# Rows of the fifth and sixth expert block transposed by VectorE and moved by DMA, table of late blocks and loads moved up

## What is computed

```python
# x, ctx_1024: (32, 128, 256) f32
x = x + xattn(ctx_1024, layernorm(x))      # 16 heads of 64, keys and values over ctx and x rows
h = layernorm(x)                           # (4096, 256)
assign = argmax(h @ centroids.T)           # one of 8 experts for each token
xhat = layernorm(h)
y = h + relu((xhat * ln_g[e] + ln_b[e]) @ w1[e].T + b1[e]) @ w2[e].T + b2[e]
alpha = sigmoid(h . centroids[e])
out = x + alpha * y + (1 - alpha) * h      # e = assign of the token
```

## Time and profile before

| | before |
|---|---|
| median of 3 runs | 1053.27 us (1052.5 to 1053.7) |
| profiled execution | 1052.73 us |
| its span, first to last instruction | 1050.9 us |
| granted TensorE clock, mean | 0.999 |
| PE busy | 1041.6 us, 99% |
| DVE busy | 844.9 us, 80% |
| ACT busy | 688.7 us, 66% |
| POOL busy | 565.3 us, 54% |
| DMA | 190.57 MB, mean 181 GB/s |

### The profile page before, as it was taken

The page is one execution under the profiler, slowest core; times in us unless marked ns, Lnnn a source line. Parts: engine busy times, 40 slices in busy tenths (PEclk is TensorE's granted clock), DMA queues, the critical chain, the costliest instruction groups (busy, mean ns, idle before and its releaser), DMA issues.

```text
span 1050.9 us, 24670 instructions
## 1 busy us (share of the span) xinstructions
PE 1041.6 (99%) x8610; PEld 940.5 (89%) x8610; DVE 844.9 (80%) x1979; ACT 688.7 (66%) x1838; POOL 565.3 (54%) x665
## 2 busy tenths in 40 slices
PE   9999999999999999999999999999999999999997
PEld 7889898988888888889898989889888999999997
DVE  7878888878888888888888879888887797767663
ACT  6765757675666767666757575766566666676761
POOL 1744464646454555545464646465444667566663
PEclk9999999999999999999999999999999999999999
DMA  6665657585757576767667585856356868777760
GB/s 212 160 169 148 170 156 189 146 215 142 201 146 197 142 193 155 200 156 197 159 168 185 142 210 137 213 144 171 91 153 196 307 198 294 250 234 234 249 194 31
DMA packets 159666, 190.57 MB, mean 181 GB/s; under 512 B 17454, under 2 KB 149038, under 8 KB 154673
## 3 DMA queue, kind: packets, MB, share of 16 engines
q1 hardware_dynamic: 155088, 179.09, 62.4%
q0 software_dynamic: 3360, 8.53, 2.2%
q10 hardware_dynamic: 1088, 1.31, 0.4%
HBM read 65.72 MB, written 46.07 MB: 106 GB/s over the span
## 4 chain that ended last, share of the span: by engine, by line
PE 96%; DVE 2%; POOL 1%; ACT 1%; DMA 0%; issue 0%; POOLq 0%; DVEq 0%
PE psum L742 17%; PE psum L775 16%; PE psum L812 11%; PE psum L902 10%; PE psum L791 10%; PE psum L827 9%; PE psum L761 8%; PE psum L938 6%; PE psum L932 5%; PE psum L830 1%; PE psum L883 1%; PE psum L914 1%; DVE neg_max L1410 1%; DMA c_in<-in_ctx_in 0%; PE psum L856 0%; DVE w_lo L1545 0%
## 5 line engine op out<-in xcount | busy, mean ns | idle before, releaser
L1823 POOL TENSOR_TENSOR prob<-prob,inv_sum 128x512 f32<-128x512 f32 x172 | 177.7, 1047 | 190.1 <-DVE inv_sum L1416 189.2
L1133 ACT ACTIVATE prob<-psum,neg_max 128x256 f32<-128x256 f32 x344 | 160.2, 478 | 38.8 <-DVE neg_max L1410 38.5
L1410 DVE TENSOR_REDUCE neg_max<-psum 128x2 f32<-128x512 f32 x256 | 161.9, 672 | 27.7 <-PE psum L791 27.5
L1422 DVE STREAM_TRANSPOSE prob<-prob 128x512 f32<-128x512 f32 x172 | 118.5, 698 | 12.3 <-POOL prob L1823 11.9
L1823 POOL TENSOR_TENSOR w_ring<-w_ring,inv_sum 128x512 f32<-128x512 f32 x76 | 78.1, 1041 | 76.0 <-DVE inv_sum L1416 75.7
L1140 ACT ACTIVATE head_out_hi<-psum 128x512 fp32r<-128x512 f32 x52 | 31.1, 597 | 105.6 <-PE psum L812 102.4
L1119 ACT ACTIVATE v_n<-psum 128x512 f32<-128x512 f32 x128 | 77.9, 608 | 26.7 <-PE psum L775 22.7
L1108 ACT ACTIVATE k_hi<-psum 128x512 fp32r<-128x512 f32 x128 | 77.0, 603 | 22.0 <-PE psum L742 21.3
L1461 DVE TENSOR_TENSOR k_lo<-psum,k_hi 128x512 fp32r<-128x512 f32 x128 | 85.7, 674 | 0.0
L742 PE MATMUL psum<-kv_t_hi,w_hi 128*128 128x512 f32 x252 | 85.0, 419 | 0.0
L775 PE MATMUL psum<-w_hi,kv_t_hi 128*128 128x512 f32 x256 | 80.2, 395 | 0.4 <-DVE k_lo L1461 0.4
(11 more groups left out here) (215 smaller groups left out, 2952.4 us busy)
## 6 DMA issues: line engine op xcount, KB each, us to landing
sorted_rows<-filler SPq DMA_DIRECT2D x54, 660.0 KB
prob_t<-prob SPq DMA_DIRECT2D x172, 128.0 KB, 2.8
w_ring<-prob SPq DMA_DIRECT2D x172, 128.0 KB, 2.7
w<-in_experts SPq DMA_DIRECT2D x19, 1024.0 KB, 7.8
w_ring<-in_experts SPq DMA_DIRECT2D x18, 1024.0 KB, 6.7
prob_t<-w_ring SPq DMA_DIRECT2D x76, 128.0 KB, 2.8
w_ring<-w_ring SPq DMA_DIRECT2D x76, 128.0 KB, 2.7
w_ring<-normed SPq DMA_DIRECT2D x56, 128.0 KB, 3.0
```

The costliest lines, as they stand in the source:

```text
L1133: act.activation(prob_at(u, bb)[:, :, parity, i], scores_i, ACT.Exp, bias=neg_max[:, at, i:i + 1], accum_out=prob_sum[:, at, i:i + 1]).the ...
L1410: dve.tensor_reduce(neg_max[:, (4 * u + n) % 8, :], psum[:, n, :].rearrange("p (i j) -> p i j", i=2), AXIS_X, ALU.max, negate=True).then_i ...
L1422: dve.transpose(probs, probs).then_inc(s_quad, 1)
L1823: pool.tensor_tensor(probs, probs, inverse, ALU.mult).then_inc(s_soft, 1)
```

## The change

TensorE's transposes of blocks 4 and 5 go; these two blocks take the way of the later ones. `transpose_rows(4)` stands after `split_xn(3)` on VectorE, `transpose_rows(5)` after `split_hidden(3)`. `late_blocks()` moves up: before `low_weights_1(4)` instead of after `split_xn(4)`; `split_xn(4)` comes ahead of `split_hidden(3)`. On SyncE, `move_rows(4)` stands between the loads of block 5's first weights and block 4's second weights; the loads of the rows of blocks 6 and 7, which need the late table, come before `move_rows(5)`, the first weights of block 6, and the second weights of block 5. In `bank_order` two `ft` entries become `pass` entries.

```diff
+FIRST_MOVED = 4
 def bank_order:
-    order += [("ft", 3), ("fy", 1, 0), ("fy", 1, 1), ("rank", n_pairs - 1), ("total",), ("ft", 4),
-              ("fy", 2, 0), ("fy", 2, 1)]
-    for slot in range(3, n_slots):
-        order += [("ft", slot + 2) if slot + 2 < n_early else ("pass", slot, 0), ("fy", slot, 0), ("fy", slot, 1), ("pass", slot, 1)]
+    order += [("ft", 3), ("fy", 1, 0), ("fy", 1, 1), ("rank", n_pairs - 1), ("total",)]
+    for slot in range(2, n_slots):
+        order += [("pass", slot, 0), ("fy", slot, 0), ("fy", slot, 1), ("pass", slot, 1)]
 wait_rows_moved, move_rows, normalise_rows, row_gain_bias, split_xn:
-    ... n_early ...
+    ... FIRST_MOVED ...
 SyncE, for s in range(2, n_early):
                     load_weights_1(s)
+                    if s == n_early - 1:
+                        move_rows(FIRST_MOVED)
                     load_weights_2(s - 1)
                     load_b2(s - 1)
-                load_weights_2(n_early - 1)
-                load_b2(n_early - 1)
                 scattered(n_batches)
                 run = block_steps(sp, count_empty(sp))
                 run(n_early, (load_rows,), (load_vectors,))
                 run(n_early + 1, (load_rows,))
+                for s in range(FIRST_MOVED + 1, n_early):
+                    move_rows(s)
                 run(n_early, (load_weights_1,))
+                load_weights_2(n_early - 1)
+                load_b2(n_early - 1)
                 run(n_early + 1, (load_weights_1,))
 TensorE:
                 layer_1(3)
-                row_transposes(4)
                 layer_2_split(2)
                 for s in range(3, n_early):
                     layer_1(s + 1)
-                    if s + 2 < n_early:
-                        row_transposes(s + 2)
                     layer_2_split(s)
 VectorE:
                 split_xn(3)
+                transpose_rows(4)
                 finish(1)
                 read_ranks(n_pairs - 1)
                 places(n_batches - 2)
                 places(n_batches - 1)
+                late_blocks()
                 low_weights_1(4)
+                split_xn(4)
                 split_hidden(3)
-                split_xn(4)
-                late_blocks()
+                transpose_rows(5)
                 finish(2)
                 for s in range(3, n_early):
-                    if s + 2 == n_early:
-                        transpose_rows(s + 2)
                     low_weights_1(s + 2)
                     split_hidden(s + 1)
                     split_xn(s + 2)
-                    if s + 3 > n_early:
-                        transpose_rows(s + 3)
+                    transpose_rows(s + 3)
                     finish(s)
```

More of the change, by code:

```diff
@@ L35, with bank_order @@
 NW, NW2, NR, NBLOCK = 2, 3, 4, 7
+FIRST_MOVED = 4
 FIRST_SPLIT = 1
 W_OUT_PIECES = 4
-def bank_order(n_pairs, last_of_early, n_early, n_slots):
+def bank_order(n_pairs, last_of_early, n_slots):
     n_steps = 4 * n_pairs
@@ L129, in build @@
     assert last_of_early % 2 == 1
-    assert 5 <= n_early <= n_sure - 2
-    order = bank_order(n_pairs, last_of_early, n_early, n_slots)
+    assert FIRST_MOVED + 2 <= n_early <= n_sure - 2
+    order = bank_order(n_pairs, last_of_early, n_slots)
     number = {item: i for i, item in enumerate(order)}
@@ L446, in wait_rows_moved @@
             def wait_rows_moved(eng, s):
-                eng.wait_ge(f_xm[s % 2], 4 * 16 * ((s - n_early) // 2 + 1))
+                eng.wait_ge(f_xm[s % 2], 4 * 16 * ((s - FIRST_MOVED) // 2 + 1))
             def wait_high(eng, g, side):
@@ L547, in move_rows @@
                 def move_rows(s):
-                    sp.wait_ge(f_xt, s - n_early + 1)
-                    if s == n_early:
+                    sp.wait_ge(f_xt, s - FIRST_MOVED + 1)
+                    if s == FIRST_MOVED:
                         wait_made(sp, ("wout", n_batches - 1))
                     else:
-                        sp.wait_ge(f_g, s - n_early)
+                        sp.wait_ge(f_g, s - FIRST_MOVED)
                     for a in range(4):
@@ L1175, in normalise_rows @@
                         wait_inputs_moved(act, n_pairs - 1)
-                    elif s < n_early + 2:
+                    elif s < FIRST_MOVED + 2:
                         wait_made(act, ("ft", s - 2))
@@ L1182, in normalise_rows @@
                         src, dst = row[:, 0:d_model], xhat[:, s % 2, i, :]
-                        if s >= n_early:
+                        if s >= FIRST_MOVED:
                             src = src.rearrange("p (c k j) -> p j c k", c=KC, j=4)
@@ L1191, in row_gain_bias @@
                     item = ("ft", s)
-                    if s < n_early:
+                    if s < FIRST_MOVED:
                         wait_made(act, item)
@@ L1622, in split_xn @@
                 def split_xn(s):
-                    if s < n_early:
+                    if s < FIRST_MOVED:
                         wait_read(dve, ("ft", s))
                     else:
-                        dve.wait_ge(f_g, s - n_early + 1)
+                        dve.wait_ge(f_g, s - FIRST_MOVED + 1)
                     if s >= 3:
```

## The result

| | before | after |
|---|---|---|
| median, beside each other | 1053.17 us (1052.5 to 1053.7, 10 runs) | 1055.31 us (1054.08 to 1056.68, 10 runs) |
| ratio | | 1.0018, 95% interval [1.001, 1.0026] |
| profiled execution | 1052.73 us | 1054.08 us |
| its span | 1050.9 us | 1052.2 us |
| granted TensorE clock, mean | 0.999 | 0.998 |

The change made the kernel 2.1 us slower in the median, where I had forecast 0.5 us faster and a range up to 1054.8. The two profiled executions differ by 1.35 us, so the profiles explain that much and no more.

The account below looks back on a forecast made before the run. TensorE (PE), busy 1041.6 of 1050.9 us, was taken to bound the kernel. Profiled: 1052.73 - 0.84 + 0.2 + 0.1 = 1052.2 us; the median lay 0.54 above the profiled execution, so forecast 1052.7, range 1051.9 to 1054.8.

Parts of the forecast that it names:

- What bounds the kernel: Whole run: TensorE is busy 1041.6 of 1050.9 us and never late among the blocks; other engines have slack.
- PE's saving, 2 x 0.42: On TensorE: one set of four transposes costs 0.42 us of period; two sets go, saving 0.84 us.
- VectorE up to `layer_1(4)`: Critical place: split_xn(4) ends at 856.3 or 856.5, PE wants it at 856.57; stall 0.2 us, ends 0 and 3.
- the second case: GpSimd's subtraction lands ahead of low_weights_1(4) or split_xn(4): PE stalls 1.8 to 3.0 us, net +1.0 to +2.2; chance 0.2.
- "softer" row: Trace row: split_xn(4)'s subtraction ended at 853.79, before GpSimd's base rows did; by it a meeting costs next to nothing.
- Moved rows of block 4: They land between 847.8 and 852.0, taken as 849; ScalarE comes at 851.17: no wait, at the upper end 0.8 us.
- Block 5: At layer_1(5): split_xn(5) ends at 868.4, just in time, stall 0 to 0.3 us; ScalarE waits some 1.5 us.
- SP's queue behind it: Block 5's second weights go out near 864.5 instead of 857.34, land by 873, needed after 877: hidden, cover 4 us.
- Slower: Chance 0.07 that the median comes out slower by more than 2.1 us, about 0.2%, the limit of measurement.

Follow-up runs that it names:

- e7: Kernel before with one wait added: TensorE's layer_1(12) waits until VectorE has finished block 10; 1054.49 us, ratio 1.0013.
- e15: e5 again on another chip: rows moved, VectorE's and SP's orders old, GpSimd's five waits; 1052.55 us, ratio 0.999.
- e2: Changed kernel with one wait added: GpSimd starts low_weights_2(3) only when split_xn(4) is done; 1054.62 us, ratio 1.0012.
- e4: Kernel before with VectorE's order alone changed: late_blocks ahead of low_weights_1(4), split_xn(4) ahead of split_hidden(3); 1054.96 us, ratio 1.0015.
- e6: Changed kernel with e5's five waits, block 5's second weights back ahead of the table, move_rows(5) ahead of block 7's rows; 1053.59 us, ratio 1.0002.
- e10: Changed kernel with GpSimd's low_weights_2(s) waiting for split_xn(s + 1) for s = 4 to 7 only; 1054.7 us, ratio 1.0004.
- e16: e2 once more, for another profile: changed kernel with GpSimd's one wait at block 3; came out at 1053.48 us.
- e5: e3 with five waits added: GpSimd's low_weights_2(s) waits for split_xn(s + 1), s = 3 to 7; 1052.27 us, ratio 0.9987.
- e9: Changed kernel with e5's five waits of GpSimd, blocks 3 to 7, and nothing else changed; 1054.15 us, ratio 1.0004.
- e12: e5 with block 6's first weights issued ahead of its vectors and block 7's rows; 1052.35 us, ratio 0.9988.
- e13: e5 with VectorE's order alone as in the change (table up), SP's order old; 1059.26 us, ratio 1.0053.
- e14: e5 with SP's order alone as in the change, VectorE's order old; 1058.14 us, ratio 1.0037.
- e1: Changed kernel unedited, run again for a second profile; 1057.4 us, ratio 1.004 against the kernel before.
- e11: Changed kernel unedited, run again on a third chip; 1054.23 us, ratio 1.0005 against the kernel before.
- e3: Changed kernel with only the rows moved: VectorE's order and SyncE's loads as in the kernel before, no waits; 1054.18 us, ratio 1.0008.

## Why the prediction was wrong

**What bounds the kernel.** Right. TensorE's idle time of 2.0 less 0.84 makes 1.16 of the 1.36 us; the rest is the slower start after an idle time, which e7 shows as well (1.3 for 1.1).

**PE's saving, 2 x 0.42.** Right: the periods to `layer_1(5)` and on are 12.15 and 12.09 where before had 12.51 and 12.09, and e15's span is 0.8 below before's.

**VectorE up to `layer_1(4)`: the step that failed.** I took a stall of 0.2 with ends 0 and 3; it was 2.0. Its terms were good: the table took 4.45 us (848.49 to 852.94; I had 4.16) and ended at 852.9 (852.8). What failed was the order of the two engines. I had GpSimd's subtraction arrive near 854 and held back by `low_weights_1(4)`, "if it is first", and counted that as protection. It arrived at 853.14, because the base rows began at 852.01, not 852.4, and took 1.08 us, not the 1.58 that they had taken beside `split_xn(4)`; it was held back, as reckoned; but it then stood ahead of `split_xn(4)`'s cast and took 2.2 us from it. So the second case (chance 0.2) came true with its mechanism, price (1.8 to 3.0) and net (+1.0 to +2.2; +1.36 in the profiled execution, 2.1 in the medians), while its condition, a table 1.2 us late, was wrong: the subtraction need only arrive during `low_weights_1(4)`. By my own placing of both it had to. e2 (the wait takes it away) and e4 (the table alone brings it) show this.

I had weighed the rule of the Trainium skill (SBUF — State Buffer, "Who interferes with whom"), by which the engine that comes second waits for the whole instruction of the first. The rows agree with it in both directions: 2.1 us of GpSimd's standing, 2.2 of VectorE's. The "softer" row against which I set it was a meeting with `base` rows, and I misread it: those are two short instructions, 0.61 and 0.98 us there and 0.55 undisturbed, while the subtraction took 0.93 instead of 0.69. Each could stand only for the rest of a short one, so the row says little on a meeting with one of 2.4 us and should not have lowered the chance.

**Moved rows of block 4.** Right: ScalarE took them at 851.03 without waiting.

**Block 5.** I had a wait of ScalarE of 1.5 and the split done by 868.4; measured 1.19 and 869.36, with PE 1.38 behind, thanks to its own stall. Where that stall is gone (e2), the slack is 0.10, as the sum had it ("just in time"), and the meeting is at `split_hidden(3)`, which the prediction had named as possible.

**SP's queue behind it.** Half wrong. Second weights of block 5 were hidden, as said. That they, now at 865.63, lie close ahead of block 6's moved rows, I did not price: these landed 6.3 us after issue, and block 6's slack fell from 2.7 to 0.2 us. That load is not the whole of it: with it back in its place (e6) the wait for the moved rows is gone, but one of 3.50 for block 6's first weights stands there and the slack is 0.10; with both old orders (e15) it is 1.3. I stopped at block 5; e10's 1.49 and e16's 0.42 at `layer_1(6)` are the cost.

**Range and chances.** "Slower" had 0.07 and the top was 0.5 us too low. Of the 2.1 us, 1.36 is shown in profiles. For the rest the runs give candidates, not shares: a clock at its lower level for 3.4 us (+1.5, seen in one profile of the three with the idle time), and stalls at blocks 5 and 6. The clock has a mark in the timed executions too: of the changed kernel's first 16, seven had a mean granted clock of 0.997 or less, and they took 1055.48 to 1059.71 us; of the 103 of the kernel before in the four groups, none was below 0.998. The median's distance from before is itself not the same everywhere: 1.0018, 1.004 and 1.0005 in three comparisons.

**What stays open.** The change's orders with all five waits stay 1.3 us above the old ones (e6 over e5) and 1.8 (e9 over e12). The profiles go some of the way: `split_xn(4)` ends 856.53 in e6 and 854.43 in e15, against PE at 856.65 and 856.67, and e9's PE is idle 0.30 and 0.63 us at blocks 5 and 6. With the table up, the waits only move the meeting onto `split_hidden(3)` (its subtraction 2.77 to 2.79 us in e2, e6, e9, e13 and e16), ahead of `transpose_rows(5)`, which starts at 860.4 to 861.2, against 855.24 in e15; in e15 GpSimd's subtraction (854.83 to 857.24) comes when the split has ended, the transpose beside it takes its usual 0.71 us, and the table's small subtraction is held instead, which PE does not need. A wait that holds GpSimd back behind `transpose_rows(5)` as well was not tried. But e6's one profile (span 1050.5) is only 0.4 us longer than e15's; that its other executions lose more by the thin gaps is argued, not shown. e13 and e14 show that the orders can't be taken apart, not which piece of them costs it. Why e1's six executions were so much slower than e11's eleven of the same kernel (1057.4 against 1054.23 us, on two chips) is open as well.

## What to carry to other kernels

When a long instruction of VectorE is followed by the short one that TensorE waits for, a GpSimd instruction that arrives during the long one goes in between; being late for the first is no protection for the second. Work out each engine's arrival within such a pair, and hold GpSimd back with a wait where its result is needed late: five waits made 1.0008 into 0.9987 here, with the table behind. Then look where the meeting goes: with the table up it moved onto the next instructions, and the kernel stayed at 1.0002 and 1.0004. And follow a moved queue through every block that it reaches: with the new orders block 6's slack went from 2.7 to 0.2 us, one block behind the last one that I had priced.

## What was not expected of the hardware

- After an idle time of 2.0 us, TensorE's granted clock was at its lower level for 3.4 us in one of three profiles of the same kernel that have this idle time (pairs of matmuls 0.63 instead of 0.40 us); in the single profiles of e14 (3.92 us of idle) and e13 (3.49) it fell too, in those of e3 (1.89) and e10 (1.49) it did not, and with 1.1 us of idle it stayed up in eleven executions (e7).
- ScalarE stood still for 2.9 us near 853 in e9, e10, e11, e13 and e16, with a releaser that the profile only calls "remote". In e10 and e11 GpSimd's subtraction then came later and met VectorE behind the split of block 4. All five are on one chip and have the table moved up; such idle times of ScalarE, up to 4.8 us, stand in all eight profiles of that chip and in none of the others.
- An idle time cost more than itself in e7's profile: 1.1 us became 1.3, with the pair of matmuls behind it at 0.48 instead of 0.40.
